# A GNN stack on one core: norms of the node table moved to ScalarE, layer two turned one piece earlier, finishing work cut into more steps

## The reference, cut to what matters

```python
edge_index = jnp.stack([src, dst])
h = jnp.maximum(_layernorm(x, axis=-1), 0.0)
x = x + _L0_gnn_ref(h, edge_index, ...)   # gelu MLP over h[src] and h[dst] gives each edge's weight, then a GCN
h = jnp.maximum(_layernorm(x, axis=-1), 0.0)
x = x + _L1_gnn_ref(h, edge_index, ...)   # two GCN layers, 128 -> 256 -> 128
h = jnp.maximum(_layernorm(x, axis=-1), 0.0)
x = x + _L2_gnn_ref(h, src, dst, ...)     # messages by an MLP, sum over edges, update by an MLP
h = jnp.maximum(_layernorm(x, axis=-1), 0.0)
x = x + _L3_gnn_ref(h, edge_index, ...)   # three GCN layers
return x
```

## Time and profile before

| what | us |
| --- | --- |
| median of 3 runs (4226.18 to 4227.47) | 4227.3 |
| the profiled execution, its own time | 4226.57 |
| its span in the profile | 4224.8 |
| PE busy (75% of the span) | 3188.4 |
| POOL busy (54%) | 2271.7 |
| DVE busy (52%) | 2191.4 |
| ACT busy (47%) | 1995.0 |
| 832 scatters into adj (L806), busy | 1308.1 |
| 880 gathers of table rows (L798), busy | 844.0 |

### The profile page before, as it was taken

How to read it: one execution, slowest core, us unless ns; L and a number is a source line. 1 busy time by engine, 2 the same in 40 slices (tenths; PEclk the granted TensorE clock), 3 DMA queues, 4 the chain that set the end, 5 groups by cost and what they waited for, 6 DMA issues and landing times.

```text
span 4224.8 us, 68198 instructions
## 1 busy us (share of the span) xinstructions
PE 3188.4 (75%) x19727; PEld 2593.3 (61%) x19727; DVE 2191.4 (52%) x9780; ACT 1995.0 (47%) x3001; POOL 2271.7 (54%) x1856
## 2 busy tenths in 40 slices
PE   3666667644444466666899509998999999999999
PEld 2555555433333355556687407786777888888888
DVE  6666666544444599998311001247444444445444
ACT  2222222211111255555799509975555555555555
POOL 3777777777777888888888888824000000000000
PEclk8555555555555599998999859999999999999999
DMA  5999997444444599996899629974887888888897
GB/s 138 304 310 313 305 313 216 107 109 105 101 109 104 127 233 233 235 232 137 206 239 268 138 23 259 262 205 128 239 239 227 245 261 258 246 271 247 273 293 246
DMA packets 874021, 898.38 MB, mean 213 GB/s; under 512 B 186010, under 2 KB 807169, under 8 KB 873664
## 3 DMA queue, kind: packets, MB, share of 16 engines
q1 hardware_dynamic: 700656, 785.25, 59.8%
q0 software_dynamic: 168464, 107.01, 15.4%
q10 hardware_dynamic: 4544, 1.77, 0.2%
HBM read 699.91 MB, written 193.86 MB: 212 GB/s over the span
## 4 chain that ended last, share of the span: by engine, by line
PE 39%; POOL 31%; issue 13%; DVE 9%; DMA 4%; ACT 3%; SPq 0%; DVEq 0%; POOLq 0%; ACTq 0%
PE ps L1224 26%; POOL adj L806 22%; POOL rows L798 8%; PE ps L1129 5%; PE ps L1111 3%; DMA adj<-scattering 2%; ACT wide L1006 2%; DVE same L1483 2%; DVE pre L1519 1%; DVE scaled L1523 1%; DMA pieces<-adj 1%; PE ps L1286 1%; PE ps L1291 1%; PE ps L1220 1%; PE ps L1235 1%
## 5 line engine op out<-in xcount | busy, mean ns | idle before, releaser
L1224 PE MATMUL ps<-wide,tab 128*128 128x512 f32 (+2 forms) x7644 | 1724.9, 383 | 32.0 <-ACT wide L1006 15.9
L1006 ACT CAST wide<-pieces 128x1536 fp32r<-128x1536 f16 (+5 forms) x1026 | 1245.0, 1257 | 726.5 <-PE ps L1224 521.6
L1224 PEld LDWEIGHTS ps<-wide,tab 128*128 128x128 f32 x7644 | 1373.9, 189 | 336.1 <-ACT wide L1006 38.6
L806 POOL DMA_INDIRECT adj<-scattering x832 | 1308.1, 1572 | 254.9 <-issue 243.1
L798 POOL DMA_INDIRECT rows<-table,src_of x880 | 844.0, 959 | 308.7 <-issue 260.0
L1845 DVE CAST wide<-pieces 128x1024 fp32r<-128x1024 f16 (+3 forms) x604 | 398.5, 664 | 556.9 <-PE ps L1224 553.1
L1129 PE MATMUL ps<-dst_mlp,onehot_t 128*128 x2640 | 364.8, 232 | 139.3 <-DVE pre L1519 91.9
L846 POOL DMA_DIRECT2D out<-scattering x13 | 9.8, 756 | 837.3 <-DVE scattering L1805 837.3
L1129 PEld LDWEIGHTS ps<-dst_mlp,onehot_t 128*128 128x128 bf16 x2640 | 274.8, 104 | 219.3 <-issue 161.5
L1483 DVE SCALAR_TENSOR_TENSOR same<-ps,key,first_weight 128x128 bf16<-128x128 f32 x832 | 285.4, 344 | 223.5 <-PE ps L1111 223.0
L930 ACT ACTIVATE onehot<-plain,norm 128x128 f32<-128x128 bf16 x880 | 281.0, 390 | 227.6 <-DVE norm L1589 227.6
(11 more groups left out here) (259 smaller groups left out, 3316.6 us busy)
## 6 DMA issues: line engine op xcount, KB each, us to landing
pieces<-adj SPq DMA_DIRECT2D x550, 640.0 KB, 5.4
pieces<-adj SPq DMA_DIRECT2D x121, 512.0 KB, 4.7
h_rows<-rows SPq DMA_DIRECT2D x220, 256.0 KB
rows<-h_rows SPq DMA_DIRECT2D x220, 256.0 KB
onehot_list<-onehot_b SPq DMA_DIRECT2D x220, 128.0 KB, 2.8
low_row<-low_list SPq DMA_DIRECT2D x220, 128.0 KB
plain<-onehot_list SPq DMA_DIRECT2D x220, 128.0 KB
pieces<-adj SPq DMA_DIRECT2D x54, 480.0 KB, 4.6
```

Of the source, the lines that this page charges most:

```text
L806: nc.gpsimd.indirect_dma_start(out=adj[:, :], out_offset=bass.IndirectOffsetOnAxis(ap=place[:, k:k + 1], axis=0), in_=count16[:, k:k + 1], ...
L1006: nc.scalar.copy(to, of).then_inc(cast_act, 1)
L1224: last = nc.tensor.matmul(ps_sum[SUMMED[u] % 2][:, 0:b * P], tab[q % 2][:, c, half, :], of, start=(c == u0 and half == 0), stop=(kind == " ...
```

## The change

- SP stores the two edge lists after the first half of x and not after all of it.
- ACT issues its 21 later weight loads behind the node table and not ahead of it; the waits for them move behind the edge loop.
- DVE inverts the roots of blocks 0 to 23 before it measures the others, and makes `node_shift` = -mean * inverse root.
- `norm_nodes` is ACT's now: one activation per block, ReLU(x * scale + shift), straight into `h`; PE turns `h`; `copy_nodes` is a plain copy, one round later. DVE has neither L1384 nor its waits any more. `STEPS_READ` is 6 and not 8.
- In the message layer `TURN` is the place after the group's end, not the end of the next group.
- update has six steps for five: ACT norms two blocks in step 3 and two in step 4, and DVE splits in step 5. gcn3 has three for two, last two for one. The unit matrix is taken off one place earlier.

```diff
@@ tables of places
     if close:
-        turn, aux, up, down = ends[0], ends[1], ends[1], ends[2]
+        turn, aux, up, down = min(END[u] + 1, ends[0]), ends[1], ends[1], ends[2]
-    steps = {"gcn1": 2, "message": 2, "update": 5, "gcn3": 2, "last": 1}[KINDS[q]]
+    steps = {"gcn1": 2, "message": 2, "update": 6, "gcn3": 3, "last": 2}[KINDS[q]]
@@ sizes
+        node_shift = room[:, 0:NW]
-        STEPS_READ = 8
+        STEPS_READ = 6
+        ROOTS_AT = 3
@@ SP
             for k, (b0, b1) in enumerate(X_PIECES):
+                if k == len(X_PIECES) // 2:
+                    sp.wait_ge(rows_in, 16 * 6)
+                    for e in range(2):
+                        sp.dma_start(edge_list[e].rearrange("(c p) j -> p c j", p=P), rows_i[:, e, :, :]).then_inc(lists_stored, 16)
...
-            sp.wait_ge(rows_in, 16 * 6)
-            for e in range(2):
-                sp.dma_start(edge_list[e].rearrange("(c p) j -> p c j", p=P), rows_i[:, e, :, :]).then_inc(lists_stored, 16)
@@ ACT
-            for where, what in loads:
-                act.dma_start(where, what).then_inc(weights_in, 16)
-            for n, (b0, b1) in enumerate(STAT):
+            def take_node_roots(n):
+                b0, b1 = STAT[n]
                 act.wait_ge(variances, n + 1)
                 nc.scalar.activation(node_rstd[:, b0:b1], node_rstd[:, b0:b1], ACT.Sqrt).then_inc(roots_set, 1)
-            def relu_nodes(i):
+            def take_later_roots(i):
+                if i == ROOTS_AT:
+                    take_node_roots(1)
+            def norm_nodes(i):
                 b0, b1 = node_blocks(i)
-                act.wait_ge(node_fed, i + 1)
-                nc.scalar.activation(h[:, b0:b1, :], node_pre[:, i % 2, 0:b1 - b0, :], ACT.Relu).then_inc(h_set, 1)
+                act.wait_ge(node_scaled, 1 if b1 <= STAT[0][1] else 2)
+                for b in range(b0, b1):
+                    last = nc.scalar.activation(h[:, b, :], x[:, b, :], ACT.Relu, bias=node_shift[:, b:b + 1], scale=node_rstd[:, b:b + 1])
+                last.then_inc(h_set, 1)
...
-            pipeline(MC, [(2, take_first_part), (0, relu_nodes), (0, copy_nodes)])
+            take_node_roots(0)
+            pipeline(MC, [(0, take_later_roots), (3, take_first_part), (0, norm_nodes), (1, copy_nodes)])
+            for where, what in loads:
+                act.dma_start(where, what).then_inc(weights_in, 16)
...
                 for k, step in TAKE.get(t - 1, ()):
+                    if place_of(k)[-1] != "update":
+                        continue
                     if step == 2:
                         take_root()
                     elif step == 3:
-                        normalize(k)
+                        normalize(k, 0, WIDE // 2)
+                    elif step == 4 and place_of(k)[3] - place_of(k)[2] > WIDE // 2:
+                        normalize(k, WIDE // 2, WIDE)
@@ PE
-            pipeline(MC, [(0, turn_nodes), (1, multiply_nodes), (1, turn_steps)])
+            pipeline(MC, [(0, turn_nodes), (1, multiply_nodes), (2, turn_steps)])
@@ DVE
+                nc.vector.scalar_tensor_tensor(node_shift[:, b0:b1], node_moments[:, b0:b1, 0], -1.0, node_rstd[:, b0:b1], ALU.mult, ALU.mult
+                                               ).then_inc(node_scaled, 1)
...
+            invert_roots(0)
             dve.wait_ge(x_in[1], 48)
             node_stats_of(1)
-            invert_roots(0)
...
-            pipeline(MC, [(2, take_src), (0, norm_nodes), (0, read_steps), (2, split_nodes), (3, take_steps)])
+            pipeline(MC, [(0, take_src), (0, read_steps), (0, split_nodes), (3, take_steps)])
...
                 elif kind == "gcn3" and step == 0:
                     taken(nc.vector.tensor_tensor(at, of, inv, ALU.mult))
+                elif kind == "gcn3" and step == 1:
                     link(nc.vector.tensor_tensor(at, at, LAYER[q]["b"][:, :].unsqueeze(1).to_broadcast([P, many, D]), ALU.add))
                     link(nc.vector.scalar_tensor_tensor(at, at, 0.0, inv, ALU.max, ALU.mult))
...
-            clearing = {PIECE_FIRST[n] - LEAD - 1: n for n in OWN}
+            clearing = {PIECE_FIRST[n] - LEAD - 2: n for n in OWN}
```

34 lines of the change are left out of this document (14 added, 20 removed).

## The result

| | median, us | runs | lowest to highest | ratio to before, 95% interval |
| --- | --- | --- | --- | --- |
| before | 4228.29 | 20 | 4222.33 to 4241.43 | |
| after | 4241.23 | 20 | 4233.18 to 4247.76 | 1.0026 (1.0020 to 1.0033) |

The change made the kernel slower by 0.26%, about 13 us; the interval reaches from 0.20 to 0.33%. The forecast was 4206.4 with 0.9 on faster. The profiled execution of the changed kernel took 4237.48 us, its span is 4235.7, and 4235.7 - 4224.8 = 10.9 us have to be found between the two traces.

A forecast was written before the change was run, and what follows sets the result against it. POOL, never free from first gather to last scatter, and an about equally fast PE, DVE, ACT loop bound the edges, PE the layers from 2764. Front -12.6, message +1, update +3.5, gcn3 -12.5, last -0.3 give -20.9: 4206.4 us, range 4193 to 4216.

The forecast's parts named there:

- the message layer's: Message layer, turning one piece earlier: ten groups +2, head of the layer -1, together +1 us; bounds -9 and +8.
- The rival on the slow side: Edge loop start: ACT, still issuing weight loads, is late at the first one-hot copy and the kernel gets slower; chance 0.03.
- The ring: Message layer: x's return through two groups (norm, POOL additions, store, load) bounds the period, near 8.3 us despite the early turn.
- The start: Node table: first source half at 35.0 against 41.89, gain 6.9 us, or 1.1 if x is as late as its bound.
- The rounds: Node table: rounds take 33.3 us against 39.0, gain 5.7 us; bounds 2.8 and 10.7.
- The price for the norm in the Trainium skill: Node table: ACT's norm costs 293 ns by the skill's rule, not the trace's 484; as rival 4201.4 us, chance 0.08.
- Passing through: Edge loop: an earlier node table end passes through undiluted, so the last scatter comes some 12 us earlier too.
- The update layer: Update layer: ACT's 0.80 us stall goes, a 1.1 us stall behind DVE's cast comes, +3.5 us; bounds -9.3 and +15.
- gcn3 and last: Later layers: with the cast ahead of DVE's split its waits go, -12.5 us for gcn3 layers, -0.3 for the last.
- The sum: Whole kernel: all terms together -20.9 us, giving a median of 4206.4 us.

The follow-up runs named there:

- aux_first: Changed kernel, early turn kept, but ACT copies the second factor of group k before the norm of group k+1; 4212.79 us, ratio 0.9960.
- root_behind: Changed kernel, early turn kept, with ACT's square root and norm of a turned group both behind the previous group's second-factor copy; 4191.54 us, ratio 0.9912.
- turn_back: Changed kernel with layer two's turn again at the end of the next group; 4194.48 us, ratio 0.9915.
- short_add: split_later with POOL's second addition of the message layer covering only the first quarter of the columns; 4179.39 us, ratio 0.9883.
- loads_first: split_later with ACT's later weight loads moved back to the very start of its queue; 4187.64 us, ratio 0.9906.
- front_alone: Kernel before with only the node table part of the change, nothing of the layers; 4208.65 us, ratio 0.9950.
- split_later: Changed kernel with the early turn undone and seven update steps, norms in halves and the table's split in step 6; 4179.44 us, ratio 0.9889.

## Why the prediction was wrong

**The step that failed** is the message layer's: "Ten groups +2, the head of the layer -1: +1. Bounds -9 (all waits gone) and +8." It was +46.6. I asked what stands *ahead* of `normalize` on ACT ("now follows a cast of three columns and not of two") and what is moved past DVE. I did not ask what stands *behind* `take_root` and `normalize` on ACT, and so put that wait at nothing. What stands there is `copy_aux` of the group before, and PE waits for it. aux_first, root_behind and turn_back show that this is all of the loss. The upper bound came from DVE's queue alone, so it had no room for it. The rival on the slow side, late loads at the first one-hot copy, was the wrong one: the loads were issued by 76, and ACT waited for PE until its first one-hot copy at 96.89. (There are 23 of them by the traces, 28 issues with the five before them, not the 21 and 26 of the text; at about 0.5 us each it makes no difference.)

**The ring** was a mistake of another kind. That an earlier turn gains nothing and that 8.3 us stay is right for a kernel whose order on ACT is sound (root_behind), but from a wrong reason, and so by luck: short_add shortens the ring and the period stays.

**The start** was forecast at -6.9 and came to 41.89 - 32.96 = -8.9. I took half of DVE's idle time, a first measuring from 17.4, and it began at 15.72: that is 1.7 of the 2.0 us. For the second half I had let x be there, and it was. loads_first shows x as what the loads held up.

**The rounds** were forecast at -5.7 and came to -8.1. I added up durations (1.65 + 0.60 + 0.37 = 2.62). ACT's operations overlap in the rows: the copy starts 1.55 after the norms, the cast 0.47 after that, the norms 0.26 after that, 2.28 in all. The bounds of -2.8 and -10.7 held it; the first is itself 0.3 too wide, since nine rounds of 0.29 are 2.6 and leave a gain of 3.1.

**The price for the norm in the Trainium skill** was rightly left out. The Trainium skill, "VectorE: DVE Perf Modes", in its section on the TRN2 errata, has 224 cycles and the elements for ScalarE, by which I estimated 293 ns; the trace disagrees, with 490 ns for one and 0.39 us from start to start within four ((1.66 - 0.49) / 3). The round came out near the 2.2 that I estimated from the Trainium skill, but by the overlap and not by the norm's own duration.

**Passing through** held: "the prediction is wrong as a whole if the first gather moves and the last scatter doesn't", and it moved by 20.1 us for 16.8. front_alone shows it in the time, 16 to 26 us. That this is more than the 12.6 forecast is likely in part the clock in the old rounds, which was full in the one profile that I had.

**The update layer** held in mechanism, and in size by luck: +3.5 forecast, +3.5 in the stretch. I had the new stall at 1.1 us for 0.80 and the old one gone. The new one is 0.9, and by the starts of matmuls ten of the new stalls cost 10.7 us where ten of the old cost 10.1, so +0.6. The other 2.9 are what is left of the old one, 0.3 in each of ten groups. The step's reason, the order cast, second half, split, cast, is what split_later undoes.

**gcn3 and last** held in mechanism: ten of the twelve waits are gone, and two at the layer's end are left. The term was mis-sized, -12.8 for -17.4, because I took a stall for its row.

**The sum.** Without the early turn the changed kernel is turn_back, 4194.48, below my 4206.4. Its trace is 31.0 us shorter than the one of the kernel before, where I had 20.9. Against my terms 2.7 of the 10.1 come from all up to the first turning, 2.9 from the message layer, 0.3 from update, and 4.2 from the later layers, the stalls' true price.

## What to carry to other kernels

When work is moved one step earlier, write down for every engine that it touches the order of a whole step, before and after, and look at what now stands behind the moved wait; the queue that decides may be that of an engine for which nothing seems to have moved. A stall that is removed by splitting work on one engine comes back on the next unless that engine's work is moved on as well. Add up start-to-start distances and not durations, both for a round and for a stall.

## What the runs showed of the hardware

- PE waiting 3.75 us in each group of 13.8 us was followed by 6 us at a granted clock of 0.50 to 0.53 and then 1.00. In aux_first it waited 2.2 us in each group; most groups took 9.6 us, and there the same products took 1.98 us for four, but after every third wait they took 3.56 to 3.68 and the group 11.0 to 11.3. So a wait on this path cost about twice its length in one kernel, and its length in two groups of three in the other.
- The rounds of the old node table were 3.16 us apart at a granted clock of 1.00 and 4.4 to 4.6 at 0.50; in three traces the rounds took 39.0, 42.5 and 45.7 us.
- A DVE addition of 128x512 took 0.69 us by itself and 1.64 to 1.80 when it started just behind a POOL addition that was still running; a POOL addition that started 0.10 us behind one of DVE's took 1.72 for 1.27 (all in split_later).
- A wait of PE inside a run of 128x512 matmuls costs some 0.16 us more than its row says, 0.55 for 0.39, since the row counts from the end of the last matmul and not from where the next would have started; the second matmul behind it starts another 0.11 late. A wait short enough shows as none: 0.3 us a group in update.
- ACT's consecutive operations overlap: norms of 0.49 us each start 0.39 apart, and a copy of 0.58 is followed by the next operation after 0.47.
- 23 small weight loads at the start delayed the first half of x by 3.6 us, although ACT itself was not needed at that time.
